# A float32 cross-attention and FFN block: the FFN as seven block products a step, weights transposed on VectorE, one output projection block

## The reference

```python
# x [16, 112, 1024], ctx [16, 375, 1024]; all float32
q = layernorm(x) @ Wq; k = ctx @ Wk; v = ctx @ Wv        # 32 heads of 32, 8 kv heads
x = x + softmax(q k^T / sqrt(32)) v @ Wo
# FFN, 1024 -> 3584 -> 1024; act_quant divides and multiplies by the same scale
t = layernorm(x)
w = (wq.reshape(N//128, 128, K//128, 128) * w_scale[:, None, :, None]).reshape(N, K)
h = silu(t @ w1.T) * (t @ w3.T)
x = x + h @ w2.T
```

## Time and profile before

| | |
|---|---|
| median of 3 runs | 2780.91 us (2779.09 to 2782.96) |
| profiled execution | 2780.45 us, span of its instructions 2778.7 us |
| TensorE / VectorE / ScalarE / GpSimd busy | 97 / 46 / 28 / 17% |
| first projection and FFN half | 865 to 1860 us |
| second projection and FFN half | 1860 to 2776 us |
| granted TensorE clock, mean | 0.983 |

### The profile page before, as it was taken

The page is one execution under the profiler, slowest core; times in us unless marked ns, Lnnn a source line. Parts: engine busy times, 40 slices in busy tenths (PEclk is TensorE's granted clock), DMA queues, the critical chain, the costliest instruction groups (busy, mean ns, idle before and its releaser), DMA issues. The chain is left out here.

```text
span 2778.7 us, 39477 instructions
## 1 busy us (share of the span) xinstructions
PE 2703.4 (97%) x14320; PEld 2318.6 (83%) x14320; DVE 1271.1 (46%) x2198; ACT 789.0 (28%) x1452; POOL 476.7 (17%) x221
## 2 busy tenths in 40 slices
PE   7989999999987999999999999999999999999999
PEld 7978778878754788888888888878888888888888
DVE  6426777777764433333333333335433334433343
ACT  3222445444443232222222222221211211112110
POOL 1000454454552231111111111100000000000000
PEclk9999999999988999999999999999999999999999
DMA  7536555545453242222222223333211111211101
GB/s 215 166 87 162 131 142 137 145 134 137 112 123 121 98 145 106 91 91 98 98 91 91 98 103 115 95 103 113 70 67 45 60 45 46 69 51 60 45 30 53
DMA packets 184786, 277.32 MB, mean 100 GB/s; under 512 B 62368, under 2 KB 140576, under 8 KB 184720
## 3 DMA queue, kind: packets, MB, share of 16 engines
q1 hardware_dynamic: 184720, 276.43, 32.3%
HBM read 190.20 MB, written 85.72 MB: 99 GB/s over the span
## 5 line engine op out<-in xcount | busy, mean ns | idle before, releaser
L74 PE MATMUL bank<-x_h,f_w_h 128*128 128x448 f32 x1792 | 667.3, 372 | 3.1 <-DVE f_w_l L80 3.1
L76 PE MATMUL bank<-x_h,f_w_l 128*128 128x448 f32 x1792 | 657.6, 367 | 0.0
L75 PE MATMUL bank<-x_l,f_w_h 128*128 128x448 f32 x1792 | 657.4, 367 | 0.0
L74 PEld LDWEIGHTS bank<-x_h,f_w_h 128*128 128x128 f32 x1792 | 337.5, 188 | 31.6 <-DVE f_w_l L80 3.5
L76 PEld LDWEIGHTS bank<-x_h,f_w_l 128*128 128x128 f32 x1792 | 337.3, 188 | 29.7
L75 PEld LDWEIGHTS bank<-x_l,f_w_h 128*128 128x128 f32 x1792 | 337.8, 189 | 28.4
L1342 DVE TENSOR_TENSOR f_hf<-bank,f_gate 128x448 f32<-128x448 f32 x112 | 69.7, 622 | 603.0 <-PE bank L76 524.7
L1354 DVE TENSOR_TENSOR y<-bank,y 128x512 f32<-128x512 f32 x392 | 270.3, 690 | 151.1 <-PE bank L76 148.4
L691 DVE TENSOR_REDUCE a_nm<-bank 112x1 f32<-112x375 f32 x512 | 265.0, 531 | 116.8 <-PE bank L826 113.3
L74 PE MATMUL bank<-f_w_h,f_h_h 128*128 128x512 f32 x784 | 312.5, 399 | 0.0
L76 PE MATMUL bank<-f_w_h,f_h_l 128*128 128x512 f32 x784 | 306.4, 391 | 0.0
(11 more groups left out here) (105 smaller groups left out, 3919.0 us busy)
## 6 DMA issues: line engine op xcount, KB each, us to landing
stash<-in_L_ffn_w SPq DMA_DIRECT2D x84, 512.0 KB, 4.5
weight_scratch<-f_wt SPq DMA_DIRECT2D x84, 512.0 KB, 2.7
stash<-weight_scratch SPq DMA_DIRECT2D x84, 512.0 KB, 4.0
stash<-in_ctx SPq DMA_DIRECT2D x48, 500.0 KB
a_qst<-q_scratch SPq DMA_DIRECT2D x96, 224.0 KB, 4.8
a_kst<-k_scratch SPq DMA_DIRECT2D x96, 188.0 KB, 4.3
stash<-in_L_xattn_Wo SPq DMA_DIRECT2D x64, 128.0 KB, 4.0
q_xn<-in_x SPq DMA_DIRECT2D x16, 448.0 KB, 5.9
```

The costliest lines, as they stand in the source:

```text
L74: pe.matmul(acc, lh, rh, start=first, stop=False)
L75: pe.matmul(acc, lh, rl, start=False, stop=False)
L76: return pe.matmul(acc, ll, rh, start=False, stop=last)
```

## The change

One mixing block now covers all 14 token tiles. The residual goes to y_scratch in DRAM. The normalised, transposed x of the first half stays in SBUF unsplit (xT), that of the second goes to x_scratch. GpSimd no longer scales weights there.

gate_up replaces the first part of ffn. Its steps are mi = 0 to 55: two token halves (g) x 14 row blocks of 256 x two matrices (w1, w3). The 256 x 1024 matrix of a step is cut into 2 x 2 blocks, the 1024 x 896 activations too, and the product is made with 7 block products (Winograd's form) instead of 8: each is 4 x 3 matmuls of 448 columns. Four of the left factors are sums S of blocks of W, which GpSimd makes (sums); the right ones are sums of blocks of x, made once a half. Two products accumulate onto earlier ones in PSUM (OUT, FIRST); four banks a step, eight for two steps. VectorE adds up the rest from PSUM (add); ScalarE copies the first product (first_copy) and takes silu (gate).

In the first half a matrix is loaded so that VectorE's transposition of 32 x 32 blocks gives the whole transposed matrix: four DMAs, each to 32 partitions, in runs of 1 KB (load_raw); ScalarE scales (scale_raw), VectorE transposes (make_wT), SyncE stores it (store_wT). In the second half it is loaded back (load_wT), and the 14 blocks of w2 are prepared in the same way (load_raw2 in runs of 256 bytes, scale_raw2, make_w2T); GpSimd makes their sums (down_sums) and SyncE stores seven blocks each (store_w2). h, and four sums of its blocks that GpSimd makes (hidden_sums), go to h_scratch (store_h).

down is a third block: 7 products x 7 token tiles (MT), each 14 x 3 matmuls of 512 columns. A and B blocks are loaded, split, multiplied, and added by VectorE to y, which it has reloaded.

```diff
-        raw13 = stash[:, 0:4, :].rearrange("p (s m) n -> p s m n", s=2)
-        raw2 = stash[:, 4:6, :].rearrange("p s (n i) -> p s n i", i=P)
+        raw = stash[:, 0:2, :].rearrange("p a (c n) -> p (a c) n", n=DQ)
+        raw2 = stash[:, 0:2, :].rearrange("p a (c n) -> p (a c) n", n=2 * BL)
+        wT = stash[:, 2:6, :].rearrange("p (m r) (b n) -> p m r b n", m=2, n=P)
+        S = stash[:, 6:8, :].rearrange("p a (c b n) -> p (a c) b n", c=2, n=P)
...
+        def load_raw(sp, mi):
...
+            for q in range(Q4):
+                sp.dma_start(raw[q * BL:(q + 1) * BL, :, :], rows[q]).then_inc(raw_loaded, 16)
...
+                NM = 2 * NP
+                A_, B_, C_, D_ = ([bank[j], bank[j + 4]] for j in range(4))
+                OUT = [A_, B_, D_, C_, A_, B_, C_]
+                FIRST = [True, True, True, True, False, True, False]
...
+                        for mi in range(2 * NM):
+                            if mi == 2:
...
+                                sp.dma_start(xT[:, :, :], x_scr).then_inc(x_loaded_, 16)
+                            if mi >= 2 and mi % 2 == 0:
+                                store_h(mi // 2 - 1)
+                            if mi >= NM + 2 and mi % 2 == 0:
+                                store_w2((mi - NM) // 2 - 1)
+                            if mi >= NM - 1 and mi % 2 == 1 and mi + 1 < 2 * NM:
+                                load_raw2((mi + 1 - NM) // 2)
+                            if NM <= mi + 2 < 2 * NM:
+                                load_wT(mi + 2)
+                            if mi + 2 < NM:
+                                store_wT(mi + 2)
+                                if mi + 3 < NM:
+                                    load_raw(sp, mi + 3)
...
                     @block.gpsimd
...
+                        for mi in range(2 * NM):
+                            if mi >= 2 and mi % 2 == 0:
+                                hidden_sums(mi // 2 - 1)
+                            if mi == NM - 2:
+                                x_sums(1, False)
+                            if mi == NM - 1:
+                                x_sums(1, True)
+                            if mi + 2 < 2 * NM:
+                                sums(mi + 2)
+                            if mi > NM and mi % 2 == 1:
+                                down_sums((mi - NM) // 2)
...
                     @block.scalar
...
+                                if nxt:
+                                    split_w(mi + 1, i)
...
+                                if i == 2 and mi + 2 < NM:
+                                    scale_raw(mi + 2)
+                                if i == 3 and mi >= NM and mi % 2 == 0:
+                                    scale_raw2((mi - NM) // 2)
...
                     @block.vector
...
+                                if i >= 3 and mi + 2 < NM:
+                                    make_wT(mi + 2, i - 3)
+                                if i < 4 and mi >= NM and up:
+                                    make_w2T((mi - NM) // 2, i)
...
                     @block.tensor
...
+                                for k in range(KH):
+                                    last = split_product(
+                                        pe, OUT[i][m][:, 0:TB],
+                                        (WH[:, i, k, :], WL[:, i, k, :]),
+                                        (XH[:, i, k, :], XL[:, i, k, :]),
+                                        FIRST[i] and k == 0, k == KH - 1, not FIRST[i])
...
+        def down():
...
+                        sp.wait_ge(b_stored, 112 * NP)
+                        load_b(0, 0)
...
+                        load_a(0)
...
+                        load_b(0, 1)
+                        load_a(1)
...
+                                    sp.dma_start(y[at:at + n, r, t, :], y_scr[tok:tok + n, :]
...
         queries()
         attention()
...
+        with nc.sbuf_tensor("xT", [P, KT, HALF], f32) as xT:
+            mixing(xT)
+            gate_up(xT)
+        down()
```

More of the change, by code:

```diff
@@ L50, in build_program @@
     TB = HALF // 2
-    TT = HALF // P
+    NT_TOK = TOK // P
+    NP = NI // 2
+    KH = KT // 2
+    Q4 = 4
+    BL = P // Q4
+    DQ = D // Q4
+    MT = HALF // P
     FB = 512
@@ L1115, in _ @@
                                     last.then_inc(o_done, 1)
-                        def step(t, slot, use):
-                            products(t, slot)
-                            transposes(t - 1, 1 - slot)
-                        tiles(pe, step)
-                        transposes(TT - 1, 0)
-        def ffn(half, y, x2_h, x2_l):
+                        for t in range(1, NT_TOK):
+                            products(t)
+                            transposes(t - 1)
+                        transposes(NT_TOK - 1)
@@ L1442, in pair @@
-                        def pair(p, more):
-                            for par in range(2):
-                                for tb in range(2):
-                                    gate_up(p, par, tb, more)
-                            pe.wait_ge(t_lo, t2_first(p, 1) + T2)
-                            for t in range(TT):
-                                down(p, t)
-                                if more and t < T13 and half == 0:
-                                    transpose13(p + 1, 1, t)
```

1067 lines of the change are left out of this document (649 added, 418 removed).

## The result

The changed kernel takes 2834.54 us (median of 4 runs, 2829.54 to 2836.68) against 2780.0 of the kernel before on the same chip: a ratio of 1.0192, 95% interval 1.0174 to 1.021. The prediction was 2880 us, slower, range 2650 to 3000. The profiled execution has a span of 2832.3 us. First the page after: span, busy times, and the chain that ended last.

A forecast was written before the change was run, and what follows sets the result against it. Waiting in two load-and-store loops, not TensorE, was taken to bound gate/up. Mixing 1044.5, gate/up 1323 and down 512 summed to 2879.5 in the span, stated as 2880 us, 3.6% slower, range 2650 to 3000.

The forecast's parts named there:

- mixing ends: Projection block before gate/up: old end at 959.0, seven more tiles 82.5, last store 3, so 1044.5 us.
- start-up until matrix 2 is transposed: Start of gate/up: VectorE's scaling wait, transposes, x sums and splits, GpSimd in the way 3, together 40.5 us.
- first loop: Gate/up, first token half: store, load, scaling and VectorE in series, 20.4 us a step against TensorE's 17.0; 25 turns, 510.
- turn to the second token half: Between gate/up's token halves: x sums on GpSimd, seven VectorE splits, fourth-sum wait, first w2 load: 56.4 us.
- second loop: Gate/up, second token half: waits through GpSimd, SyncE's queue and VectorE, 52.2 us a pair against TensorE's 34.1; 13 turns, 679.
- last steps and stores: End of gate/up: last step and a half 27, last hidden sums and stores 10 us.
- down: Third block: first matmul at 14.6, tile 2 at 46.3, 47 tiles x 9.58, six block changes, last store: 512 us.
- TensorE's savings: Whole kernel: fewer gate/up and down matmuls, no weight transposes, one Wo load and split saved: 296 us less TensorE work.
- the rival of the dear transpose: VectorE transpose in gate/up costs 1.3 us, not 0.62, adding 68 and 35 us: 2985 us; chance 0.12.
- The signs: Traces: TensorE waiting on WL splits each step, 20 us scalings, 52 us pairs, even load behind w2 stores, down gap 10.
- TensorE sets the pace in both halves: Gate/up: first loop under 17.0 us, second under 34.1, so TensorE's own work decides: 2537 us; chance 0.12.
- Shorter loops: Gate/up: overlapping transfers or GpSimd passes of 0.95 us give loops of 19.0 and 44 us: 2740 us; chance 0.21.

The follow-up runs named there:

- e5: Changed kernel with raw loads ahead of the store, both second-half matrix loads first in their step, down's residual loaded tile by tile: 2569.1 us.
- e8: e5 with a step's transposes in two pairs, two second-half x sums made in pieces during the first half, down's first a ahead of b: 2542.7 us.
- e1: Changed kernel with the load of raw matrix k+1 issued ahead of the store of matrix k in the first token half: 2763.2 us.
- e4: Changed kernel with down's residual loaded tile by tile instead of 7.3 MB ahead of a for tile 2: 2818.0 us.

## Why the prediction was right, and where its steps were off

The sign and the mechanism were right; the time was 45 us too high. Part of the closeness is luck: the terms below that were too low, by 38 us together, made up for nearly half of the 85 us by which others were too high. In the span of the profiled executions, step by step (forecast, measured, difference):

| | forecast | measured | difference |
|---|---|---|---|
| mixing ends | 1044.5 | 1042.7 | -2 |
| start-up until matrix 2 is transposed | 40.5 | 54.5 | +14 |
| first loop, 25 turns | 510 (20.4) | 518.5 (20.7) | +8 |
| turn to the second token half | 56.4 | 46.6 | -10 |
| second loop, 13 turns | 679 (52.2) | 615.1 (48.1, the first 38.3) | -64 |
| last steps and stores | 37 | 52.4 | +15 |
| down | 512 | 502.5 | -10 |

**TensorE's savings** held nearly: 17.0 us a step are what e5 shows in its second loop and e8 in its first, where nothing else is in the way, and a tile of down takes 9.52 us (9.58 forecast) in every trace. e8 is 239 us faster than before, and its trace shows TensorE's waits of 30 us in the start-up of gate and up, 6 at the turn and 23 at the start of down, 59 in all, of which the kernel before had some 12 at the starts of its two FFN halves. So some 285 of the 296 us are accounted for. One term was a little too large: of the 83 us between the two halves of the kernel before, from which I took 80 for the transposes, some 11 are the distance of its matmuls, 0.207 us in the first half and 0.203 in the second, on 2688 of them.

**The first loop** was right link by link: 10.4 us from the last transpose's store to the scaling (9.7 forecast), scaling 2.6 (2.2), and the rest VectorE's. That one queue serves in order, which I had assumed, is shown by e1: the store's 3 us came off in full. The transpose cost 0.70 us (0.62 taken, bounds 0.4 to 1.3); the rival of the dear transpose is dead.

**The second loop** had every link where it was forecast. With X the odd matrix's landing, Y the even one's and M the issue of raw w2: X to Y 27.6 (30.8), Y to M 8.9 (10.1), M to X' 11.1 (11.3). Of the 4.1 us by which a turn is shorter, 2.6 are GpSimd's, the term that was too dear: 17.6 us for the twelve passes, not 20.2. Alone they take 1.28 and 1.13, 14.8 in sum, where I had 16.0 with waits on itself; the hindrance by VectorE's splits was 2.8 us, not 4.2. I had let each of seven splits hold GpSimd for its full length; in the trace it is shared, some of the wait falls on the split. (The hindrance that the prediction names adds up to 77 us, not to the 90 that it gives for all of it.) The first turn was a miscount: no w2 block is stored yet, so it takes 38.3 us.

**Two more terms were miscounted**, both too low. Behind the last w2 load two and a half steps remain, not one and a half: 15 us. In the start-up, 14 us: VectorE makes four sums of x there, not three; its passes of 1792 elements took 3.1 instead of 2.0 beside GpSimd's sums, where I had put 3 us in all; three times it waits 1.8 us for ScalarE's split of a sum just made; and ScalarE's copy of the first product stands in its order behind the last split of x, so that TensorE waits 8.8 us for it. Why the turn between the token halves was 10 us shorter than forecast, I have not traced. Down's six block changes, 2 us each in the forecast, cost nothing: no tile behind them took longer than 9.52 us. The gap ahead of tile 2 was there (12.75 us, 10 forecast), and e4 shows its cause.

**The signs** it had named: steps of 20 us, the even load right behind the w2 stores, GpSimd passes that are at times long, and the gap in down were seen. One was wrong: TensorE waits for a sum on VectorE (207.5 us), and within the two loops never for a weight split. The load is behind both; but whoever had looked only for a wait on WL would have missed it, since the instruction that TensorE waits for is not the one that is late.

**The rivals.** "TensorE sets the pace in both halves" had been given 0.12 and 2537 us; it is what the same instructions do in another queue order (e5, profiled at 2562.5; e8 at 2548.1). "Shorter loops", 19.0 and 44, is not what happened: the first was 20.7, and the second, 48.1, lay between its 44 and the forecast's 52.2. Its cheap GpSimd pass of 0.95 us is dead; one alone takes 1.28.

## What to carry to other kernels

Where no engine is full and the bound engine has small gaps in every turn, write the turn down as a circle (landing, passes, stores, issue, landing) with its times: the sum of the links is the period, and what counts is which link waits for which buffer and queue place. Loads that the next step needs go ahead of stores that nobody waits for; but a single buffer ties a store into the circle as firmly as the queue does, so after a cut, look for the second circle before adding up its gain. An instruction moved off the circle helps only if what it waits for comes early enough: the same exchange of two lines on GpSimd gave 76 us in one queue order and 10 in another.

## What the runs showed of the hardware that I had not expected

**A short VectorE split can wait through a whole GpSimd pass.** At the turn of e5, GpSimd makes sums of 1792 elements; VectorE's split of 512, 0.67 us alone:

```profile
1557.29 5.71 POOL L1301 TENSOR_TENSOR stash<-xT,g_t 128x1792 f32<-128x1792 f32 x1
...
1559.02 4.54 DVE L90 TENSOR_TENSOR g_WL<-stash,g_WH 128x512 fp32r<-128x512 f32 x1
```

It ends 0.6 us behind the GpSimd pass. The adds with one operand in PSUM keep their 0.61 us beside GpSimd (as at 2005.56 and 2007.26 of the changed kernel), the transposes their 0.70 and ScalarE's splits their 0.63; only VectorE's instructions with two SBUF inputs grew, from 0.67 to between 1.0 and 1.4 in the second loop. The Trainium skill, "SBUF — State Buffer", section "Who interferes with whom", says that a VectorE instruction with two SBUF inputs contends with a GpSimd one that reads SBUF, and that one with at most one SBUF input does not, outside the modes that use both ports. By that rule, these rows agree. The prediction counted the xn pass of the earlier trace rows, 2.27 us instead of 0.81, among the rows that agree with the rule of the two inputs; it reads only one tensor from SBUF, so that this rule does not explain that row. What to take from it: long GpSimd passes may be worth cutting in pieces, even where their sum does not change. e8 does so at the turn, where TensorE's waits fall from 16 us in e5 to 6, but it moves part of the passes away as well, so that the share of the pieces is not shown.

**After an idle stretch TensorE runs at half clock.** The changed kernel around the wait of 8.7 us shown above; the clock is the third figure from the end of each row:

```profile
2027.00:2031.50 4.50, 0.00 (x0) 0.00 (x0) 2.26 (x3) 0.63 (x1) 2.87 (x3) 0.50 0.17 73
2031.50:2034.00 2.50, 2.43 (x7) 2.20 (x8) 1.83 (x3) 1.89 (x4) 2.50 (x2) 0.50 0.00 0
2037.00:2041.00 4.00, 4.00 (x22) 3.70 (x21) 4.00 (x8) 0.63 (x1) 0.00 (x0) 1.00 0.73 123
```

It had stood idle from 2022.8; the granted clock was 0.50 (1.2 GHz) from 2027 to 2034 and 1.00 (2.4 GHz) again from 2037. Matmuls between are 0.37 us apart instead of 0.2026, some 2 us a pair. In the second loop I take it to cost nothing, since no link of the circle is a product of TensorE's; the mean of 0.90 would then be a consequence of the gaps and not a cause of the time. That is argued from the links, not tried. In down, where TensorE sets the pace, it did cost: tile 2, behind the wait of 12.75 us, took 2.5 us longer than the tiles behind it.

**SyncE's own issuing was a link.** Four stores of w2 sums take 2.54 us to issue and four loads of raw weights 3.1 to 4.7: in the second loop's 47.5 us, the queue spends 4.1 us issuing seven stores that are ready, and the even load stands behind them.
